# A graph network layer on one core: rows, low halves and coordinates ahead of norm 2, and three results left in PSUM

## The reference

```python
h = jnp.maximum(_layernorm(x, axis=-1), 0.0)
# layer 1, on h (mask is adj)
xc = transpose(h)
c = relu(bn(conv1d(xc, conv1_w, pad 0)))
c = bn(conv1d(c, conv2_w, pad 8))                # 17 taps
x_conv = relu(c + xc), transposed back
s = h @ w_se.T + b_se                            # 3 coordinates
dist = sq[:, :, None] + sq[:, None, :] - 2.0 * einsum('bnd,bmd->bnm', s, s)
A = exp(-dist) * adj
x_nmp = A @ relu(h @ w_msg.T + b_msg)
# gates r, z, n of a GRU from [x_conv, x_nmp] and h
x = x + (1 - z) * tanh(gi_n + r * gh_n) + z * h
# layer 2
h = jnp.maximum(_layernorm(x, axis=-1), 0.0)
x = x + adj @ (h @ weight) + bias
```

## Time and profile before

| | |
|---|---|
| median of 3 runs | 363.3 us (362.76 to 363.44) |
| profiled execution | 363.2 us, span 361.3 us |
| TensorE matmul busy | 334.4 us, 93% of the span |
| VectorE, ScalarE, GpSimd busy | 276.7, 223.7, 158.2 us |
| mean granted TensorE clock | 0.981 |
| DMA | 15.02 MB, mean 42 GB/s |

### The profile page before, as it was taken

The page is one execution under the profiler, slowest core; times in us unless marked ns, Lnnn a source line. Parts: engine busy times, 40 slices in busy tenths (PEclk is TensorE's granted clock), DMA queues, the critical chain, the costliest instruction groups (busy, mean ns, idle before and its releaser), DMA issues.

```text
span 361.3 us, 6315 instructions
## 1 busy us (share of the span) xinstructions
PE 334.4 (93%) x2196; PEld 300.8 (83%) x2196; DVE 276.7 (77%) x733; ACT 223.7 (62%) x431; POOL 158.2 (44%) x130
## 2 busy tenths in 40 slices
PE   8699969998999899989999899989999999989865
PEld 6589858788988798879988898879989998889664
DVE  5697996898779878888679878889679877643671
ACT  2958635878575875588466876578468825352342
POOL 7061540037912495137903494229801791172121
PEclk9999989999999999999999999999999999999986
DMA  7800200001300121002200121002000000000001
GB/s 243 302 3 0 90 0 0 2 1 59 115 4 1 32 87 60 0 1 80 98 1 0 32 94 53 2 0 90 30 0 2 31 29 0 3 29 32 0 1 58
DMA packets 7951, 15.02 MB, mean 42 GB/s; under 512 B 1008, under 2 KB 1648, under 8 KB 7792
## 3 DMA queue, kind: packets, MB, share of 16 engines
q1 hardware_dynamic: 7776, 14.62, 12.0%
q10 hardware_dynamic: 144, 0.01, 0.0%
HBM read 10.43 MB, written 4.19 MB: 40 GB/s over the span
## 4 chain that ended last, share of the span: by engine, by line
issue 39%; POOL 28%; PE 17%; DVE 9%; ACT 6%; POOLq 0%; DVEq 0%; ACTq 0%
POOL rs L1258 4%; POOL px L922 3%; POOL base L1312 3%; POOL base L1315 3%; POOL px L912 2%; POOL ac L918 2%; POOL base L1308 2%; POOL px L915 2%; POOL rs L1253 2%; POOL x_ring L1300 2%; POOL base L1306 2%; PE pNR L482 1%; DVE work L1033 1%; PE pZ L476 1%; PE pP L337 1%
## 5 line engine op out<-in xcount | busy, mean ns | idle before, releaser
L1258 POOL TENSOR_TENSOR rs<-ve,neg_half 128x4 f32<-128x4 f32 x16 | 16.2, 1011 | 87.5 <-DVE ve L1063 87.5
L1253 POOL TENSOR_TENSOR rs<-ve,neg_half 128x8 f32<-128x8 f32 (+1 forms) x9 | 15.5, 1721 | 81.0 <-DVE ve L942 81.0
L297 PE MATMUL pP<-cx_hi,conv_hi 128*128 128x256 f32 x154 | 45.0, 292 | 0.0
L299 PE MATMUL pP<-cx_hi,conv_lo 128*128 128x256 f32 x154 | 43.4, 282 | 0.0
L298 PE MATMUL pP<-cx_lo,conv_hi 128*128 128x256 f32 x154 | 43.4, 282 | 0.0
L297 PE MATMUL pQ<-cx_hi,conv_hi 128*128 128x256 f32 x126 | 37.7, 299 | 0.0
L298 PE MATMUL pQ<-cx_lo,conv_hi 128*128 128x256 f32 x126 | 35.4, 281 | 0.0
L299 PE MATMUL pQ<-cx_hi,conv_lo 128*128 128x256 f32 x126 | 35.4, 281 | 0.0
L715 ACT ACTIVATE work<-work,nb,rs 128x128 f32<-128x128 f32 x60 | 24.7, 483 | 9.7 <-DVE nb L1067 9.7
L297 PEld LDWEIGHTS pP<-cx_hi,conv_hi 128*128 128x128 f32 x154 | 29.1, 189 | 0.3
L298 PEld LDWEIGHTS pP<-cx_lo,conv_hi 128*128 128x128 f32 x154 | 29.1, 189 | 0.3
(11 more groups left out here) (261 smaller groups left out, 1087.2 us busy)
## 6 DMA issues: line engine op xcount, KB each, us to landing
x_ring<-x_in SPq DMA_DIRECT2D x16, 256.0 KB, 2.9
adj_ring<-adj_in SPq DMA_DIRECT2D x16, 256.0 KB, 3.1
out<-x_ring SPq DMA_DIRECT2D x15, 256.0 KB, 2.0
work<-conv_in SPq DMA_DIRECT2D x1, 1088.0 KB, 7.7
x_ring<-gate_in SPq DMA_DIRECT2D x1, 576.0 KB, 8.9
out<-x_ring SPq DMA_DIRECT2D x2, 128.0 KB, 1.7
early<-early_in SPq DMA_DIRECT2D x1, 129.5 KB, 3.4
late<-late_in SPq DMA_DIRECT2D x1, 128.0 KB, 8.7
```

Of the source, the lines that this page charges most:

```text
L297: pe.matmul(acc, w_hi, m_hi, start=start, stop=False)
L299: return pe.matmul(acc, w_lo, m_hi, start=False, stop=stop)
L1253: pool.tensor_tensor(rs1[:, lane], ve1[:, lane], neg_half[:, lane], ALU.pow).then_inc(rs1_set, 1)
L1258: pool.tensor_tensor(rs2[g % 2][:], ve2[g % 2][:], neg_half[:, 0:GG], ALU.pow).then_inc(rs2_set, 1)
```

## The change

Three kinds of edits.

1. *Order in steps.* VectorE: `hidden_lo(b)` and `coordinates(a)` come ahead of `normalise2(pp)`, `right_rows(a)` ahead of `normalise2(qq)`. ScalarE: `left_rows(a)` comes ahead of `scaled_first` and `conv1_out(b)`.
2. *Results in PSUM.* The exponential overwrites the distances in their bank, and the mask product reads them there and writes `att` in SBUF; the wait for the neighbour sums moves from the exponential to the mask. `conv_out` writes in place into pQ and pP, which ScalarE and VectorE then read. Two transposes of TensorE wait for `att_set` (the mask) where they waited for `exp_set`.
3. *Opening.* ScalarE writes h_hi and hT of groups 0 and 1 first and `hn` later (`hidden_graphs`), with a wait for the low half. VectorE builds the pair rows of group 3 ahead of the low half of the sums of group 1. GpSimd's third to fifth sums wait for these pair rows.

```diff
@@ two transposes of TensorE, rows_turn and o_turn
                 elif g > 1:
-                    have(pe, exp_set, g)
+                    have(pe, att_set, g)
...
                 if g % 2 == 0:
-                    have(pe, exp_set, min(g + 4, NG))
+                    have(pe, att_set, min(g + 4, NG))
@@ ScalarE
-            def hidden(g):
+            def hidden_graphs(g):
                 have(act, hT_placed, g + 1)
+                have(act, hlo_set, g + 1 if g < 2 else 0)
                 act.activation(hn[g % 2][:].rearrange("p (g n) -> p g n", g=GG),
...
             def decay(g):
                 have(act, dist_done, g + 1)
-                have(act, nmp_done, g - 1)
-                act.activation(att[g % 2], dist_bank(g)[:], ACT.Exp, scale=-1.0).then_inc(exp_set, 1)
+                act.activation(dist_bank(g)[:], dist_bank(g)[:], ACT.Exp, scale=-1.0).then_inc(exp_set, 1)
...
-                act.activation(xc_hi[:, 2 * e:2 * e + 2], base[e][:], ACT.Relu).then_inc(xchi_set, 1)
+                act.activation(xc_hi[:, 2 * e:2 * e + 2], phases(e), ACT.Relu).then_inc(xchi_set, 1)
...
-                hidden(0)
-                hidden(1)
+                hidden_rows(0)
+                hidden_rows(1)
                 place_bias(0)
+                hidden_graphs(0)
                 conv1_out(0)
+                hidden_graphs(1)
                 act.wait_ge(conv_loaded, 16)
...
                 second(pp)
+                if front:
+                    left_rows(a)
                 if middle:
                     scaled_first(t)
                 if front:
                     conv1_out(b)
-                    left_rows(a)
@@ VectorE
             def masked(g):
...
                 have(dve, exp_set, g + 1)
-                dve.tensor_tensor(att[g % 2], att[g % 2], adjs(g), ALU.mult).then_inc(att_set, 1)
+                have(dve, nmp_done, g - 1)
+                dve.tensor_tensor(att[g % 2], dist_bank(g)[:], adjs(g), ALU.mult).then_inc(att_set, 1)
...
-                dve.scalar_tensor_tensor(base[e][:], (pQ, pP)[e][:].rearrange("p (s h w) -> p s h w", s=2, h=2),
-                                         bn_a[:, 1:2], base[e][:], ALU.mult, ALU.add).then_inc(ct_set, 1)
+                dve.scalar_tensor_tensor(phases(e), phases(e), bn_a[:, 1:2], base[e][:], ALU.mult, ALU.add).then_inc(ct_set, 1)
...
-                dve.scalar_tensor_tensor(xc_lo[:, 2 * e:2 * e + 2], base[e][:], 0.0,
+                dve.scalar_tensor_tensor(xc_lo[:, 2 * e:2 * e + 2], phases(e), 0.0,
...
                 right_rows(2)
+                pair_rows(3)
                 sums_lo(1)
-                pair_rows(3)
                 masked(2)
...
+                if front:
+                    hidden_lo(b)
+                    coordinates(a)
                 normalise2(pp)
                 if front:
-                    coordinates(a)
-                    hidden_lo(b)
                     pair_rows(a)
...
                 residual(qq)
+                if front:
+                    right_rows(a)
                 normalise2(qq)
-                if front:
-                    right_rows(a)
                 shift2(qq)
@@ GpSimd
-                for k in range(1, 6):
+                pre(pool, 1, 1)
+                pre(pool, 1, 2)
+                pool.wait_ge(pair_set, 4)
+                for k in range(3, 6):
                     pre(pool, 1, k)
```

More of the change, by code:

```diff
@@ L203, in two, with phases @@
             return t[:, 2 * e * N:2 * (e + 1) * N]
+        def phases(e):
+            return (pQ, pP)[e][:].rearrange("p (s h w) -> p s h w", s=2, h=2)
         def turn_bank(g):
@@ L657, in first, with hidden, hidden_rows @@
                 last.then_inc(hn_set, 1)
-            def hidden(g):
+            def hidden_graphs(g):
                 have(act, hT_placed, g + 1)
+                have(act, hlo_set, g + 1 if g < 2 else 0)
                 act.activation(hn[g % 2][:].rearrange("p (g n) -> p g n", g=GG),
                                turn_bank(g)[:].rearrange("p (n g) -> p g n", g=GG), ACT.Relu).then_inc(hG_set, 1)
+            def hidden(g):
+                hidden_graphs(g)
+                hidden_rows(g)
+            def hidden_rows(g):
+                have(act, hT_placed, g + 1)
                 act.activation(half(h_hi, g), turn_bank(g)[:], ACT.Relu).then_inc(hhi_set, 1)
@@ L1189, in step @@
                 residual(qq)
-                normalise2(qq)
                 if front:
                     right_rows(a)
+                normalise2(qq)
                 shift2(qq)
```

## The result

| | before | after |
|---|---|---|
| median, measured together | 363.31 us (360.86 to 364.69, 20 runs) | 365.37 us (363.94 to 366.92, 20 runs) |
| ratio, with 95% interval | | 1.0058 [1.0043, 1.0074] |
| profiled execution | 363.2 us, span 361.3 | 364.42 us, span 362.5 |
| TensorE, VectorE busy | 334.4, 276.7 us | 333.5, 254.4 us |

The change makes the kernel 1.6 to 2.7 us slower. The forecast was 365.3, in a range of 362.5 to 366.9. VectorE's busy time fell by 22 us, and that bought nothing.

The account below looks back on a forecast made before the run. TensorE was taken as the bound, busy 282.4 of 294.1 us between 51.86 and 346 us. Steps +1.7 and +1.1, opening -2.5, start +0.3, clock fall +1.5 sum to +2.1: 363.2 becomes 365.3 us, range 362.5 to 366.9.

Parts of the forecast that it names:

- What is late next: In the steps, the pair-row transpose would wait for the mask product, 1.5 to 1.9 us in six places.
- The size in the steps: Net lengthening of the steps by the later mask product: +1.7 us for five steps, +1.1 us for step 6.
- +0.34: Each of five steps longer by 0.34 us, as the transpose runs at 85.34 against 85.00 in step 1.
- the hand-over to TensorE: In the steps, the pair-row transpose would start 0.05 us after the mask product ends.
- the 0.12 allowed for its wait: In step 1, VectorE's low half of h goes first and waits 0.12 us for ScalarE's hT.
- Step 6: VectorE waits 0.90 us for hT in place of 0.12, so the transpose runs at 285.23, not 284.11: +1.1 us.
- End of the opening: Pair rows of group 3 come first, so its distances run at 49.07, not 51.44: -2.5 us.
- PSUM at nothing: Mask products and convolution outputs using PSUM operands would cost nothing, the mask product taking 0.69 us.
- The start: Moving hn of group 0 back makes ScalarE's chain, and with it direct(0), 0.27 us later: +0.3 us.
- the fall of 1.5 us: At the start, TensorE's clock falls to half behind about 2.16 us idle ahead of direct(0): +1.5 us, bounds 0 and 1.7.
- the rival without a fall: No fall of TensorE's clock at the start: 363.8 us, no measurable change; chance 0.28.
- The rival "faster": In the steps, the waits go and nothing replaces them: 352.6 us in full, 358 with half; chance 0.15.

Follow-up runs that it names:

- e2: The changed kernel with right_rows(a) behind normalise2(qq) again: 359.75 us, ratio 0.9941 to the kernel before.
- e1: The changed kernel with the exponential written to SBUF again and both transposes waiting for exp_set: 364.33 us, ratio 1.0037 to the kernel before.
- e7: The changed kernel with the old order of VectorE and GpSimd at the end of the opening, mask still from PSUM: 369.41 us, ratio 1.0177 to before.
- e8: The kernel before with only the convolution outputs left in PSUM: 362.94 us, ratio 0.9982 to the kernel before.
- e9: The kernel before with only the exponential left in PSUM, mask reading it there, transposes waiting for the mask: 363.73 us, ratio 1.0032 to before.
- e5: The changed kernel with twelve idle matmuls in place of six at the start: 365.43 us, ratio 1.0059 to the kernel before.
- e3: The changed kernel with coordinates(b) and pair_rows(b) between normalise2(qq) and shift2(qq): 359.29 us, ratio 0.9891 to the kernel before.
- e4: The changed kernel with pair rows of b ahead of shift2(qq) and the exponential in SBUF with the old waits: 357.75 us, ratio 0.9852 to before.
- e12: The changed kernel, exponential in PSUM only for groups 0 to 3, pair rows and group 3 left rows earlier, twelve idle matmuls: 353.87 us, ratio 0.9730 to before.

## Why the prediction was right, point by point

- **What is late next: right.** The transpose of the pair rows waits for the mask, 1.63 to 2.01 us in six places (1.5 to 1.9 predicted), the waits of the earlier trace rows are gone from the steps, and shift2 waits 1.12 us for the power (1.1).
- **The size in the steps: too small.** Of the +0.34 the parts on VectorE hold: in step 1 the mask starts 9.14 us behind the low half, where it stood 8.42 behind the statistics, +0.72. The step of the sum that was mis-sized is the hand-over to TensorE. The transpose was to start 0.05 us behind the mask's end and starts 0.14 behind it (0.83 us from the mask's start, not 0.74), in every step: 0.45 us in steps 2 to 6. Then the next low half comes up to 0.09 us later than the 0.12 allowed for its wait (30.66 us behind the transpose, at 113.50; before 30.45 to the statistics at 115.45). It is 0.09, 0.05, 0.02 and 0.02 in the first four, so it is not the price of a transpose that had waited; e2, whose transpose mostly has no wait, shows the same 30.6. Steps 2, 3 and 5 measure +0.54, +0.48 and +0.46. Step 4 has +0.74: VectorE idles 0.19 us ahead of its mask, without a releaser in the trace. It did so before too (0.20), but then the transpose came 0.95 us behind the mask's start, TensorE didn't wait for it, and it cost nothing. Step 6 is +1.30, not +1.1. In sum +3.5 for +2.5.
- **End of the opening: right,** -2.55 for -2.5, and the clock did not fall there. The reason was half: e1 and e7 show that the mask from PSUM and the new order carry each other.
- **PSUM at nothing: right in the steps** (e8, e9: 199.1), wrong in the opening in both directions, as e9 (+0.5 us up to `distances(3)`, +0.2 up to step 1) and e1 (the SBUF mask +0.3, then half clock) show.
- **The start: +0.11 for +0.3, and the fall of 1.5 us charged in full** where it shows in three profiles of seven, with about 1.5 us each time. The change's own profile has none, so what it shows is the rival without a fall (363.8), with steps that cost 1.0 us more. That is why its sum is +1.2; the medians say +2.1. The surplus of 0.9 us fits falls in about half of the executions, but e5 says that they are not, or not alone, those at the start. This stays open.

So 365.3 for 365.4 is partly luck. In the profile the steps were 1.0 us too cheap and the fall 1.5 us too dear, and 0.9 us of the medians, which no single profile places, fill the gap. The rival "faster" needed 1.6 us less on VectorE between blend and mask. e3 found 1.13 of it by covering the power, and e4 and e12 the rest by not waiting for the mask. I had argued that there was no slow operation to free, and had not asked which operation could be moved under the power.

## What to carry to other kernels

Before an operation is moved forward, see what it covered: 0.7 us of right rows beside another engine's 1.0 us power were free, and ahead of it they cost their full length. Leaving a result in PSUM changes who may overwrite the bank: follow the next writer of the bank and read its wait against the new last reader, in the steps and in the opening apart, since one place may gain (beside GpSimd) what the other loses. Ask for each new wait which independent work could fill it; with two calls moved (the pair rows of b, the left rows of group 3), the exponential in PSUM in the opening alone and six more idle matmuls at the start, the same edits were 2.7% faster, not 0.6% slower.

## What was not expected of the hardware

- TensorE's clock fell to 0.50 (1.2 GHz) behind 2.1 us without work in three profiles of seven of nearly the same program, and cost about 1.5 us each time; behind 0.8 to 1.2 us in none of seven. Behind the 2.15 us near the end it fell within 1.5 us in eight of fourteen. In the steps of the change it did not fall behind waits of up to 2.01 us. So about 2 us of idle time may cost or not.
- An exponential that reads and writes one PSUM bank takes the same 0.59 us as with its result in SBUF, and `conv_out` in place 0.75 us for 0.74. The Trainium skill, "VectorE: DVE Perf Modes", section "The TRN2 errata", charges a PSUM source 62 cycles more, an estimate of 0.065 us. The mask products of the change, with one source in PSUM, take 0.68 to 0.69 us, those of before at their shortest 0.681, so that surcharge is not seen.
- VectorE's small operations took 0.17 to 0.19 us beside GpSimd's power on 128x4 (1.01 us) in e3, and 1.15 to 1.42 us beside its sums (1.4 us) in e7.
